# A transformer chain on one core: shorter quantisation and top-2, P.V once per head pair, a ring of 12 tiles and shared buffers

## The reference, cut to what matters

```
x += 0.5 * L0_ffn(ln(x))      # FP6 quantisation per 32-block of x and of the weight, then x @ w.T + b
x += L0_attn(ln(x))           # one head, causal, K and V projected, plus its own input
x += 0.5 * L0_ffn(ln(x))
x += 0.5 * L1_ffn(ln(x))      # 16 heads of 64, non-causal, with expert gates
x += L1_attn(ln(x))           # Mamba-like: projections, conv, scan over 16 states, gating
x += 0.5 * L1_ffn(ln(x))
```

```
q, k = x Wq[h], x Wk[h];  proj_v[e] = x Wv[e]
gate_v = x Ws  [512, 16 heads, 8 experts];  w, sel = top_2(gate_v)
v[h] = sum over the 2 chosen e of sigmoid(w) * proj_v[e]
attn[h] = softmax(q k^T / 8) v[h]
mask_o = one_hot(top_2(x Wd));  res = sum over h, e of mask_o * attn[h] Wo[e]^T
```

## Time and profile before

| what | value |
|---|---|
| profiled execution | 2787.38 us, its span 2785.5 us |
| TensorE (PE) busy | 2584.8 us, 93% of the span |
| TensorE weight loads (PEld) | 1716.1 us, 62% |
| VectorE (DVE) | 2181.1 us, 78% |
| ScalarE (ACT) | 1853.1 us, 67% |
| GpSimd (POOL) | 737.0 us, 26% |
| mean granted TensorE clock | 0.965 of full speed |

### The profile page before, as it was taken

How to read it: one execution, slowest core, us unless ns; L and a number is a source line. 1 busy time by engine, 2 the same in 40 slices (tenths; PEclk the granted TensorE clock), 3 DMA queues, 4 the chain that set the end, 5 groups by cost and what they waited for, 6 DMA issues and landing times.

```text
span 2785.5 us, 51284 instructions
## 1 busy us (share of the span) xinstructions
PE 2584.8 (93%) x17437; PEld 1716.1 (62%) x17437; DVE 2181.1 (78%) x3233; ACT 1853.1 (67%) x4430; POOL 737.0 (26%) x564
## 2 busy tenths in 40 slices
PE   4699999989999999999899999999999999999997
PEld 3566675665666756666565666656566665666665
DVE  7588786989799798988987888797788868775552
ACT  3265755857687676866766767686677768666563
POOL 1000000434145124603540343164145315410000
PEclk9699999999999999999999999999999999999998
DMA  3425354564565546555563654556466564545423
GB/s 135 114 85 132 93 147 100 140 183 112 148 156 161 137 124 178 136 136 152 145 165 103 169 155 137 149 167 176 112 172 169 132 164 141 167 122 147 108 80 91
DMA packets 753407, 385.77 MB, mean 138 GB/s; under 512 B 421568, under 2 KB 678656, under 8 KB 752768
## 3 DMA queue, kind: packets, MB, share of 16 engines
q1 hardware_dynamic: 747104, 380.66, 50.7%
q10 hardware_dynamic: 6048, 1.84, 0.3%
HBM read 274.91 MB, written 115.87 MB: 140 GB/s over the span
## 4 chain that ended last, share of the span: by engine, by line
PE 62%; DVE 21%; issue 9%; ACT 3%; DMA 2%; POOL 2%; SPq 1%; ACTq 0%; DVEq 0%; POOLq 0%
PE ps L723 13%; PE ps L732 11%; PE ps L745 11%; PE ps L792 8%; PE ps L712 6%; DVE h_ring L1234 6%; PE ps L798 4%; DVE h_nmax L1054 3%; PE ps L805 2%; DVE h_ring L1244 2%; PE ps L764 1%; POOL h_ring L659 1%; PE ps L832 1%; ACT h_prob L899 1%; DVE h_wide_a L1206 1%
## 5 line engine op out<-in xcount | busy, mean ns | idle before, releaser
L899 ACT ACTIVATE h_prob<-ps,h_nmax 128x512 f32<-128x512 f32 x1024 | 710.0, 695 | 134.6 <-DVE h_nmax L1054 132.7
L1054 DVE TENSOR_REDUCE h_nmax<-ps 128x2 f32<-128x1024 f32 x512 | 621.3, 1213 | 147.4 <-PE ps L723 147.1
L732 PE MATMUL ps<-ident,h_prob 128*128 128x128 f32 x4096 | 623.1, 279 | 26.3 <-DVE h_probT L1295 13.5
L732 PEld LDWEIGHTS ps<-ident,h_prob 128*128 128x128 f32 x4096 | 480.7, 144 | 197.0 <-issue 118.5
L723 PE MATMUL ps<-h_qk 64*128 64x512 f32 x2048 | 592.1, 655 | 0.5 <-ACT h_prob L899 0.3
L668 POOL TENSOR_TENSOR h_wide_c<-h_wide_c,h_ring 128x512 f32<-128x512 f32 x240 | 331.3, 1381 | 734.3 <-DVE h_ring L1244 734.3
L1019 ACT ACTIVATE h_probT<-ps 128x512 f32<-128x512 f32 x796 | 478.5, 601 | 61.6 <-PE ps L732 59.2
L745 PE MATMUL ps<-h_probT,h_v_sb 128*64 128x256 f32 x4096 | 504.0, 389 | 5.4 <-DMA h_v_sb<-v_d 3.2
L745 PEld LDWEIGHTS ps<-h_probT,h_v_sb 128*64 128x64 f32 x4096 | 273.8, 138 | 314.0 <-issue 147.0
L1234 DVE TENSOR_TENSOR_SCAN h_ring<-h_ring 128x512 f32<-128x512 f32 x256 | 395.1, 1543 | 36.2 <-POOL h_ring L659 20.2
L659 POOL TENSOR_TENSOR h_ring<-h_m_xpad,h_m_b_rows 128x512 f32<-128x512 f32 x256 | 348.9, 1373 | 257.5 <-DVE h_m_xpad L1354 250.1
(11 more groups left out here) (222 smaller groups left out, 2669.3 us busy)
## 6 DMA issues: line engine op xcount, KB each, us to landing
h_mix_diag<-mix_blocks SPq DMA_DIRECT2D x128, 512.0 KB, 3.8
v_d<-h_v_mixed SPq DMA_DIRECT2D x128, 256.0 KB, 4.2
h_v_sb<-v_d SPq DMA_DIRECT2D x128, 256.0 KB, 3.3
at_d<-h_att SPq DMA_DIRECT2D x128, 256.0 KB, 2.9
h_mo_diag<-mo_blocks SPq DMA_DIRECT2D x128, 256.0 KB, 3.5
h_att<-at_d SPq DMA_DIRECT2D x128, 256.0 KB, 3.7
h_m_b_rows<-dbl_d SPq DMA_DIRECT2D x128, 256.0 KB, 4.3
h_m_c_rows<-dbl_d SPq DMA_DIRECT2D x128, 256.0 KB, 4.3
```

What stands on the lines that cost most here:

```text
L732: ins = pe.transpose(ps[:, TB + v % 2, k * P:(k + 1) * P], prob[:, v % NB, k * P:(k + 1) * P], ident[:, :])
L899: act.activation(prob[:, v % NB, :], ps[:, SB + v % 4, :], ACT.Exp, bias=nmax[:, p, j, o:o + 1], accum_out=den[:, p, j, o:o + 1]).then_inc ...
L1054: dve.tensor_reduce(nmax[:, p, j, :], ps[:, SB + 2 * w % 4:SB + 2 * w % 4 + 2, :], X, ALU.max, negate=True).then_inc(sem("row_max"), 1)
```

## The change

1. Quantisation: the exponent is taken and inverted (and, xor) in one operation, clamped to 0.5..2, and the value is scaled to steps of one, so that a single constant rounds it; the last clip is gone. 13 operations in 12 parts.
2. top-2: the first choice is written straight to `chosen`, with no copy, and `gates` is overwritten in place of g_rest; six parts a round. `chosen` has one buffer for both sets. sigmoid's 0.5 is folded into the value weights and its +1 into the product of `mix_gates`. MIX_AT falls to 30.
3. P.V: one att piece per pair p at step 8p+14 with all 8 tiles, into all 512 columns of a bank, and one copy of it. The ring `probT` has 12 tiles.
4. x_prep, x_post, nrm and nT are one buffer, x_io. The post load moves from step 14 to 20 and waits for the prep job's gates and split; the prep load waits for the store of an earlier job.

```diff
@@ quantise_part
             elif i == 4:
-                link(dve.tensor_scalar(p2.bitcast(U32), z.bitcast(U32), 0x7F800000, None, ALU.bitwise_and))
+                link(dve.tensor_scalar(p2.bitcast(U32), z.bitcast(U32), 0x7F800000, 0x7F800000, ALU.bitwise_and, ALU.bitwise_xor))
             elif i == 5:
-                link(dve.tensor_scalar(p2, p2, 1.0, 4.0, ALU.max, ALU.min))
+                link(dve.tensor_scalar(p2, p2, 0.5, 2.0, ALU.max, ALU.min))
             elif i == 6:
-                link(dve.tensor_scalar(mg, p2, ROUND, None, ALU.mult))
+                link(dve.scalar_tensor_tensor(out=mg, in0=z, scalar=4.0, in1=p2, op0=ALU.mult, op1=ALU.mult))
             elif i == 7:
-                link(dve.tensor_tensor(t, z, mg, ALU.add))
+                link(dve.tensor_scalar(p2.bitcast(U32), p2.bitcast(U32), 0x7F800000, None, ALU.bitwise_xor))
+                link(dve.tensor_scalar(t, mg, ROUND, ROUND, ALU.add, ALU.subtract))
             elif i == 8:
-                link(dve.tensor_tensor(t, t, mg, ALU.subtract))
-
+                link(dve.tensor_tensor(mg, t, mg, ALU.subtract))
             elif i == 9:
-                link(dve.tensor_tensor(mg, t, z, ALU.subtract))
+                link(dve.scalar_tensor_tensor(out=t, in0=mg, scalar=0.5, in1=t, op0=ALU.is_ge, op1=ALU.subtract))
             elif i == 10:
-                link(dve.scalar_tensor_tensor(out=mg, in0=mg, scalar=16.0, in1=p2, op0=ALU.mult, op1=ALU.is_ge))
-            elif i == 11:
-                link(dve.scalar_tensor_tensor(out=mg, in0=mg, scalar=0.125, in1=p2, op0=ALU.mult, op1=ALU.mult))
-            elif i == 12:
-                link(dve.tensor_tensor(t, t, mg, ALU.subtract))
-            elif i == 13:
-                link(dve.tensor_scalar(t, t, -FP6_MAX, FP6_MAX, ALU.max, ALU.min))
+                link(dve.scalar_tensor_tensor(out=t, in0=t, scalar=-0.125, in1=p2, op0=ALU.mult, op1=ALU.mult))
...
-        NB, PROBT = 4, 8
+        NB, PROBT, ZEROS = 4, 12, 8
-        TOP_PARTS = 7
+        TOP_PARTS = 6
...
-            "heads": [(4 * a + 10, "att", a) for a in range(HALF)] + [(8 * p + 17, "back", p) for p in range(PAIRS)]
+            "heads": [(8 * p + 14, "att", p) for p in range(PAIRS)] + [(8 * p + 17, "back", p) for p in range(PAIRS)]
...
-                                if u == 14:
+                                if u == 20:
                                     if n >= 1:
                                         sp.wait_ge(sem("x_out"), 16 * n)
-                                    sp.dma_start(x_post[:, :, :], rows(x_in[n])).then_inc(sem("x_post_in"), 16)
+                                    if n + 2 < NJ:
+                                        wait_full(sp, "gate", 1, n + 2)
+                                        sp.wait_ge(sem("nT_split"), n + 3)
+                                    sp.dma_start(x_io[:, :, :], rows(x_in[n])).then_inc(sem("x_post_in"), 16)
...
-                                    if n >= 2:
-                                        sp.wait_ge(sem("normed"), n)
-                                    sp.dma_start(x_prep[:, :, :], rows(x_in[n])).then_inc(sem("x_prep_in"), 16)
+                                    if n >= 3:
+                                        sp.wait_ge(sem("x_out"), 16 * (n - 2))
+                                    else:
+                                        wait_full(sp, "gate", 1, n - 1)
+                                        sp.wait_ge(sem("nT_split"), n)
+                                    sp.dma_start(x_io[:, :, :], rows(x_in[n])).then_inc(sem("x_prep_in"), 16)
...
+                    def attend(bank, i, p):
+
+                        pe.wait_ge(sem(f"v_in{p % 2}"), 16 * (PAIRS // 2 * i + p // 2 + 1))
+                        for a in range(2):
+                            v = UNITS * i + 8 * p + 4 * a
+                            for w in (v + 2, v + 3):
+                                wait_probT(pe, w)
+                            for k in range(J):
+                                for o in range(2):
+                                    ins = pe.matmul(bank[o * DH:(o + 1) * DH, a * 2 * P:(a + 1) * 2 * P],
+                                                    v_sb[:, p % 2, k, o * DH:(o + 1) * DH],
+                                                    probT[:, v % PROBT + o:v % PROBT + 4:2, k * P:(k + 1) * P],
+                                                    start=(k == 0), stop=(k == J - 1))
...
-                            ins = act.activation(attT[:, c % 2 * 2 * P:(c % 2 + 1) * 2 * P], bank[:, 0:2 * P], ACT.Copy)
+                            ins = act.activation(attT[:, :], bank, ACT.Copy)
...
                             if w >= PROBT:
-                                n_, a_ = divmod(w // 4 - 2, HALF)
-                                wait_full(act, "att", a_, n_)
+                                n_, p_ = divmod((w - PROBT) // 8, PAIRS)
+                                wait_full(act, "att", p_, n_)
...
                         elif part == 4:
-                            link(dve.tensor_tensor(key, key, top, ALU.is_equal))
-                        elif part == 5 and r == 0:
-                            if a == 1 and i >= 1:
+                            if r == 0 and a == 0 and i >= 1:
                                 dve.wait_ge(sem("mo_out"), 16 * i)
-                            link(dve.tensor_copy(pick, key))
-                        elif part == 5:
+                            link(dve.tensor_tensor(pick if r == 0 else key, key, top, ALU.is_equal))
+                        elif r == 1:
                             dve.tensor_tensor(pick, pick, key, ALU.add).then_inc(sem("chosen"), 1)
...
-                        link(dve.tensor_scalar(g_sig[:, :, :], g_sig[:, :, :], 0.5, 0.5, ALU.mult, ALU.add))
-                            ins = dve.tensor_tensor(mix[:, j, :, :].rearrange("p e h -> p h e"),
-                                                    g_sig[:, j, :].rearrange("p (h e) -> p h e", e=E),
-                                                    chosen[:, 0, j, :].rearrange("p (h e) -> p h e", e=E), ALU.mult)
+                            ins = dve.scalar_tensor_tensor(out=mix[:, j, :, :].rearrange("p e h -> p h e"),
+                                                           in0=g_sig[:, j, :].rearrange("p (h e) -> p h e", e=E), scalar=1.0,
+                                                           in1=chosen[:, j, :].rearrange("p (h e) -> p h e", e=E),
+                                                           op0=ALU.add, op1=ALU.mult)
```

More of the change, by code:

```diff
@@ L326, in t @@
                 return sb("h_" + name, shape, dt, at=ph)
-            x_prep = t("x_prep", [P, J, D])
-            x_post = t("x_post", [P, J, D])
-            nT = t("nT", [P, S])
+            x_io = t("x_io", [P, J, D])
+            ln["nrm"] = nrm = x_io
+            nT = x_io[:, :, :].rearrange("p j c -> p (j c)")
             nT_split = t("nT_split", [P, 2, 2, S], F32R)
@@ L441, in v_load @@
                             i_, p_ = divmod(PAIRS * i + p - 2, PAIRS)
-                            wait_full(sp, "att", 2 * p_ + 1, i_)
+                            wait_full(sp, "att", p_, i_)
                         sp.dma_start(v_sb[:, p % 2, :, :], rows(v_d[i])[:, :, p * PW:(p + 1) * PW]
@@ L483, in zero_blocks @@
                     def zero_blocks():
-                        zeros = probT[:, :, :].rearrange("p n s -> p (n s)")
+                        zeros = probT[:, 0:ZEROS, :].rearrange("p n s -> p (n s)")
                         sp.wait_ge(sem("zeros"), 1)
@@ L734, in turn_probs @@
                         ins.then_inc(sem("turned"), 1)
-                    def attend(bank, i, a):
-                        p, v = a // 2, UNITS * i + 4 * a
-                        for w in (v + 2, v + 3):
-                            wait_probT(pe, w)
-                        if a % 2 == 0:
-                            pe.wait_ge(sem(f"v_in{p % 2}"), 16 * (PAIRS // 2 * i + p // 2 + 1))
-                        for k in range(J):
-                            for o in range(2):
-                                ins = pe.matmul(bank[o * DH:(o + 1) * DH, 0:2 * P],
-                                                v_sb[:, p % 2, k, o * DH:(o + 1) * DH],
-                                                probT[:, v % PROBT + o:v % PROBT + 4:2, k * P:(k + 1) * P],
-                                                start=(k == 0), stop=(k == J - 1))
+                    def attend(bank, i, p):
[10 more added lines that the diff above has]
+                                                    start=(k == 0), stop=(k == J - 1))
                         return ins
@@ L761, in piece @@
                         elif what == "back":
-                            wait_taken(pe, "att", 2 * c + 1, n)
+                            wait_taken(pe, "att", c, n)
                             for j in range(J):
@@ L932, in take @@
                         elif what == "norm":
-                            if n >= 1:
```

(13 more changed lines are left out.)

44 lines of the change are left out of this document (21 added, 23 removed).

## The result

| | before | after |
|---|---|---|
| median | 2786.95 us (4 runs) | 2739.6 us (4 runs, 2730.03 to 2744.18) |
| ratio | 1 | 0.984, 95% interval 0.981 to 0.987 |
| profiled execution, its span | 2787.38, 2785.5 us | 2741.52, 2739.7 us |

What follows compares the result with a forecast made beforehand. TensorE, busy 93% of the span, was taken as the bound, with gains only from its idle time, the low clock after waits and the start: 2787.4 - 5 - 5 - 25 - 12 + 8 = 2748 us, range 2708 to 2790.

Steps and rivals of the forecast that it cites:

- D: Middle: less VectorE work, some 37 us, counting only where VectorE sets the pace; a third taken, 12 us gained, bounds 0 to 37.
- E: One P.V piece per pair of heads: its burst delays ScalarE's copies and softmax; 8 us worse, bounds 10 better to 64 worse.
- A: Start: shorter VectorE chain in quantisation, top-2 and gate product brings the first mixing earlier; 5.0 us gained, bounds 2 to 8.
- B: First attention: first P.V piece moves from step 10 to 14 and stops waiting for v; 5 us gained, bounds 0 to 7.
- C: Each job: gate product and spread two steps earlier end the value-mixing waits and slow clock; 25 us gained, bounds 0 to 45.
- TensorE's work stays: In merged P.V pieces: TensorE's work for a pair of heads remains 2 x 1.97 us in a row.
- The wait of the transposes on ScalarE: Sign against the forecast of merged P.V: waits of L732 or L723 on ScalarE or VectorE over 40 us together.
- L745's busy time still 504: Sign for the forecast: the P.V group's busy time on TensorE stays at 504 us.
- F: Shared x_io buffers: later loads cost nothing, at most 1 us a job; tail 0 to 2 us, taken as 0.
- Rival 1: Middle: VectorE or a bank is late where the mixing wait was, so little is gained; 2772 us, chance 0.18.
- Rival 3: Merged P.V: the burst starves the softmax, costing 0.6 us or more a pair of heads; 2817 us, chance 0.10.
- Rival 2: Whole kernel: everything closes, with start, mixing and VectorE gains larger and merging P.V free; 2708 us, chance 0.10.

Runs made afterwards that it cites:

- step A above: Changed kernel plus filler transposes on TensorE in the start, three at each of steps 18 to 56 and 110 ahead of the first value mixing: 2738.72 us, 0.982.
- the dummies: Dummy 512-column copies and tensor_scalars added to the changed kernel: with old quantisation 2764.43 us, 0.991; with gate product two steps later 2777.59 us, 0.994.
- the adjacent halves: Changed kernel with P.V in two half pieces, each with its own copy, both at step 8p+14: 2742.24 us, 0.983.
- the split one: Changed kernel with P.V in two pieces again, att a at step 4a+10, with 256 columns and a copy for each: 2731.37 us, 0.978.

## Why the prediction came out as it did

The forecast was 2748 us, the median is 2739.6, in the range and on the side that was given 0.78. The sum held better than its terms: D was too small, E was near by a cancellation, and some 12 us of the gain were not traced to a step.

- **A, −5 by the first mixing: right in mechanism, lost to the clock in both executions of the changed kernel that were profiled.** The kernels with the same start and no fall of the clock begin the first mixing at 105.8 to 106.4 us, 4 us before the 110.27 of before. In the profiled execution the clock fell and two pieces took 3.05 us longer (0.91 and 2.14); the forecast had no term for that. How much of the 5 us reaches the end stays open (step A above).
- **B, −5: plausible, not tested alone.** The wait for v is gone, and 10.3 us are gained by the first marker. That 10 were forecast for A and B together is luck, as A's part was lost in this execution. The undo runs of C and of VectorE's work have this marker at 391.9, 395.6 and 397.0, so most of the 10.3 us are from neither.
- **C, −25: right in place and size.** The waits on issue are gone, the load follows the spread, and undoing it costs 20 to 24 us. More of it is busy time than idle time (17.3 or 22.7 of some 30 us between the markers), as its second price, the clock, says.
- **D, −12: the term that was mis-sized.** The step was "I take a third"; the third rested on VectorE being full in few stretches. All of VectorE's work put back, A's share with it, costs 21 to 25 us for 43.8 us; the quantisation alone 13 to 17 for 26.6; the dummies 8 to 10 for 17 to 23. Each is about half. By the forecast's own terms the same work was to bring 3.6 in the start and 12 in the middle, 16 in all. Of the quantisation the work was also priced low, 1.4 us each where 26.6 / 16 = 1.7 were measured. Each price has the 9 us of uncertainty, so a third is not excluded for the dummies alone. C was charged with the clock and D was not; the rows at 1802 us show that this can matter, but the division into idle and busy is too rough to give a factor: in the runs that undo C, D and the quantisation the busy time grew by 1.4 to 1.6 us for each microsecond of idling against one execution of the changed kernel (17.3 to 12.5, 15.3 to 9.7, 11.8 to 8.7), and by 3 to 5 against the other (22.7 to 7.4, 20.7 to 4.7, 17.2 to 3.7).
- **E, +8: right in sign and near in size** (6 to 14, 11 against the adjacent halves), wrong in mechanism. "TensorE's work stays" failed: it has 0.16 us a pair less, some 20 us, so the burst costs about 30 us in waits and clock (20 and the net 10), not 8. The wait of the transposes on ScalarE, which was to show it, did not rise (7.6 us in the changed kernel, 10.2 in the split one, whose row is not shown). What rose is the wait for the norm, 26.8 against 18.1, and for ScalarE's copies into aT, 7.6 against 1.9 (row not shown). How the burst makes these late was not tested.
- **"L745's busy time still 504": wrong,** 471.3, in part real (some 20 us) and in part records that overlap.
- **F, 0:** no wait of the load at step 20 shows, the tail is 0.1 us off.

Added up from the undo runs: C 22, all of VectorE's work 23, less 10 for E, is 35, where 47 was measured. The undo of C and of the dummies add up without overlap; the undo of all three at once was not run. The 12 us that are missing are no more than the errors of such a sum, and B is in none of its terms.

Rival 1 (2772) fell with C: nothing took the mixing wait's place. Rival 3 (2817) would have needed 0.37 us a pair; E's 6 to 14 us are 0.05 to 0.11. Rival 2 (2708) was right that D was underpriced, but D and A together came to 21 to 25 us and not to its 36, E took its share, and TensorE's idle time stayed at 102.5 us.

## What to carry to other kernels

Ask of every wait of the pacing engine, and not just of the longest, whether its clock falls behind it; the rows of the clock tell, the length of the wait does not. An engine that is busy 78% on average can still be worth half a microsecond of time for each microsecond of its work; test it by adding dummy work to it, since moving its tasks about only moves the wait, and count the instructions on the page to see what was put back. Merging two groups of matmuls can save TensorE time and still lose: here the 20 us saved were less than the waits that the later first half brought. Read the saving from start to start, and the worth of it from markers, not from the group's busy time on the page.

## What the runs showed that was not expected

A group's busy time fell by 32.7 us, some 20 of them real, and the kernel is slower for it. In the start the same 20 matmuls took 2.47 or 4.61 us in kernels that are the same program up to there, behind waits of the same 0.90 and 0.78 us, and the first mixing followed 4 to 5 us earlier or later; what tips the clock there stays open. The two profiled executions of the changed kernel differ by 11 us at the third marker (747.0 and 736.2) and by 4 at the end.
